# Output projection of a decoder layer: one float32 product, or three float32r products on weights and activations split into two parts

## The chip, the cores and the metric

One core of a Trainium2 chip. The metric is the device time of one execution in microseconds. Everything below is about five engines of that core and their queues: TensorE (PE, with PEld for its weight loads), VectorE (DVE), ScalarE (ACT), GpSimd (POOL) and SyncE (SP). Each engine works through its own instructions in order and waits at semaphores; SyncE, ScalarE and GpSimd also issue DMAs from their in-order queues.

## The reference

A decoder layer over x of 4 x 512 x 512 (four batch rows of 512 tokens), float32. Its first part is the one that matters here:

```
xn = layernorm(layernorm(x), g_norm)
q = xn @ Wq            # 512 -> 16 heads x 128
k, v = split(xn @ Wkv) # one key and one value head
attn = softmax(16-scaled l2norm(q) . l2norm(k))
out = attn @ v         # 16 heads x 128 = 2048 columns
out = out @ Wout       # 2048 -> 512: the output projection
x = x + layernorm(out, g_out)
```

After it come a state-space scan over ctx (16 states, 512 channels, gated by the norm of x) and a mixture of 32 experts of which each token takes up to 8.

## The kernel before, in words

The four batch rows (b or r in the code) run one after another, and the expert part follows them. For each batch row TensorE makes the queries of four groups of four heads, and for every head the scores, the weighted values and the transposed output, which ScalarE evacuates as `o_t[:, h, :]` (`transposed`, line 1075). Meanwhile VectorE runs the scan: per state n a `state_input` (line 1491), a `state_scan` (1497), a `state_product` (1504) and a `state_sum` (1509), each over 128x2048, with ScalarE making the decays. States 0 to 4 run in `start_heads`, 5 to 11 in the head groups 2 and 3 (`later_heads`, 1521), and 12 to 15 in `last_states` (1538), which runs beside the output projection.

The output projection (`out_proj`, line 750) is one function per head: four tiles of 128 tokens, each one float32 product of `o_t` with `wout`, added up over 16 heads in the four banks bank_o and bank_s. The trace has two records for a float32 product. In the batch rows 0 to 2 the next row's first stages are woven between the heads, in an order written out by hand: transposes of the norm after the heads 2 and 3, keys and values after 5, the first queries after 7, the scan's input projection after 10 and 11, `scan_params` after 12, `deltas` after 13, key transposes and the other first queries after 14. The second pair of transposes waits for the first `norm_lo` (xn_lo) of VectorE. In the last batch row the 16 heads run on end, and the layer's tail (`out_copied`, norm, gates, routing) waits for them.

The weights of the projection are kept in four places of [128, 512]. SyncE loads them (`load_wout`, line 358): four heads ahead of the projection, and the others as `wout_used` says that a place is free. SyncE also loads `b_bc` and `c_bc`, the rows B and C of the states; those of states 14 and 15 stand among the weight loads (before heads 8 and 11).

GpSimd's queue holds `load_wq` (line 1909; 1 MB a group of heads, issued when the queries before it are made, since there is one place for them) and, after the fourth group of a batch row, the 32 indirect DMAs (`send`, 1916) that write the routing of the batch row before into `lists`. The first weights of the next row's queries are loaded after those sends. At the start ScalarE splits Wq into two parts (`split_wq`, 1035) and VectorE makes the rest (1443); they are stored to DRAM and loaded back by group.

Such a split is used in the kernel in many places: ScalarE rounds a value to float32r by a copy (hi), VectorE subtracts it from the value (lo), and TensorE adds up hi x hi, hi x lo and lo x hi.

## Time and profile before

| | us |
|---|---|
| median of 3 runs | 1762.98 |
| lowest, highest | 1757.42, 1764.99 |
| span of the profiled execution | 1759.8 |
| output projection stage of batch row 0 | 277.6 to 384.0 |
| the same in batch row 1, 2 | from 600.2, from 921.3 |
| output projection of the last batch row | 1242.2 to 1298 |

The profile is of one execution. A row of the timeline names the start and the length in us, the engine, the line of the kernel, the operation, what it writes and reads with its shape, how many instructions were merged, and in brackets how long the engine was idle before it and who released it. "Busy" of TensorE is modelled at its ends, and its records overlap, so a pace is read from start to start.

### The profile page before, as it was taken

The numbers are of one execution on the slowest core, as the hardware profiler recorded it, in microseconds if no ns is written. First come the engines' busy times: TensorE is split into PE (matmuls) and PEld (weight loads), VectorE is DVE, ScalarE is ACT, GpSimd is POOL, SyncE is SP. The second block draws the span as 40 slices with busy tenths as digits, with TensorE's granted clock in tenths as the row PEclk, the third lists the DMA queues.
The fourth block names the chain that finished last, engine by engine and source line by source line (L and its number), as shares of the span: only waits on it lengthen the run. The fifth ranks groups of instructions, "written<-read, shape, count | busy, mean of one in ns | idle before, by whom it ended". The sixth has DMA issues, their size and how long they took to land. (4 is left out here: it accounts for less than half of the span.)

```text
span 1759.8 us, 25049 instructions
## 1 busy us (share of the span) xinstructions
PE 1436.2 (82%) x6762; PEld 1018.9 (58%) x6763; DVE 1245.9 (71%) x1543; ACT 941.3 (53%) x2428; POOL 499.0 (28%) x307
## 2 busy tenths in 40 slices
PE   4899888988988798898869879977863746899996
PEld 1577665446766453676755357765422535677774
DVE  5465898756699975767998468699885424667663
ACT  4666662457567335675743447766320424566662
POOL 0000000000028600000880000068301545666664
PEclk9799999989999998899989989999985878999998
DMA  6692132132332422142133124212601446999985
GB/s 236 254 262 85 40 116 85 48 97 61 97 85 65 125 73 70 45 144 72 40 98 120 50 72 124 93 38 51 206 22 52 113 110 146 224 234 241 236 204 69
DMA packets 128788, 202.45 MB, mean 115 GB/s; under 512 B 44984, under 2 KB 46473, under 8 KB 127552
## 3 DMA queue, kind: packets, MB, share of 16 engines
q1 hardware_dynamic: 75120, 86.70, 17.5%
q0 software_dynamic: 27840, 63.83, 14.9%
q10 hardware_dynamic: 25744, 50.87, 9.6%
q8 instruction: 44, 0.72, 0.2%
q14 instruction: 40, 0.33, 0.1%
HBM read 170.57 MB, written 46.21 MB: 123 GB/s over the span
## 5 line engine op out<-in xcount | busy, mean ns | idle before, releaser
L1918 POOL DMA_INDIRECT lists<-entry,slot x128 | 267.8, 2092 | 227.9 <-DVE slot L1686 190.2
L1501 DVE TENSOR_TENSOR_SCAN state<-decay,dbu 128x2048 f32<-128x2048 f32 x64 | 283.1, 4423 | 24.2 <-ACT decay L1051 22.9
L1914 POOL DMA_DIRECT2D wq<-wq_dram x30 | 21.5, 720 | 869.9 <-PE pair L581 744.2
L645 PE MATMUL bank<-v_aug,probs 128*128 128x129 f32 x2048 | 253.1, 283 | 8.1 <-ACT probs L1045 8.1
L645 PEld LDWEIGHTS bank<-v_aug,probs 128*128 128x128 f32 x2048 | 244.5, 198 | 17.2 <-ACT probs L1045 16.2
L755 PE MATMUL bank<-wout,o_t 128*128 128x512 f32 x512 | 236.1, 616 | 0.0
L1045 ACT ACTIVATE probs<-bank 128x512 f32<-128x512 f32 x256 | 145.8, 605 | 106.3 <-PE bank L627 93.3
L1051 ACT ACTIVATE decay<-delta,neg_a 128x511 f32<-128x511 f32 x256 | 164.8, 736 | 65.4 <-DVE state L1501 59.4
L755 PEld LDWEIGHTS bank<-wout,o_t 128*128 128x128 f32 x512 | 100.0, 199 | 122.5 <-issue 122.1
L1953 POOL DMA_INDIRECT out<-y_ring,add_ids x68 | 125.2, 1842 | 94.8 <-DMA out<-y_ring,add_ids 66.7
L1495 DVE TENSOR_TENSOR dbu<-du,b_bc 128x2048 f32<-128x2048 f32 x64 | 146.5, 2289 | 7.0 <-DMA c_bc<-bc_dram 5.2
L1507 DVE TENSOR_TENSOR dbu<-state,c_bc 128x2048 f32<-128x2048 f32 x64 | 146.6, 2290 | 1.9
L627 PE MATMUL bank<-q_t,k_t 128*128 128x512 f32 x256 | 128.6, 640 | 13.6 <-ACT q_t L1033 9.3
L1512 DVE TENSOR_TENSOR y<-y,dbu 128x2048 f32<-128x2048 f32 x60 | 137.4, 2290 | 1.8
L579 PE MATMUL pair<-wq,xn_hi 128*128 128x512 f32 x256 | 113.6, 444 | 20.7 <-DVE q_lo L1461 16.9
L1072 ACT ACTIVATE o_s<-bank,den 128x128 f32<-128x128 f32 x256 | 73.1, 374 | 74.1 <-DVE den L1519 74.1
L1005 ACT ACTIVATE junk<-pair 128x128 bf16<-128x128 f32 x256 | 68.1, 293 | 78.9 <-PE pair L581 78.8
L580 PE MATMUL pair<-wq,xn_hi 128*128 128x512 f32 x256 | 107.4, 420 | 0.0
L581 PE MATMUL pair<-wq,xn_lo 128*128 128x512 f32 x256 | 107.2, 419 | 0.0
L503 PE MATMUL bank<-const,o_s 128*128 128x128 f32 x272 | 47.7, 303 | 72.1 <-ACT o_s L1072 72.1
L1858 DVE TENSOR_TENSOR xt_lo<-pair,xt_hi (+1 forms) x70 | 48.1, 689 | 80.7 <-ACT xt_hi L1317 79.8
L875 PE MATMUL bank<-w_hi,xt_hi 128*128 x272 | 99.0, 364 | 6.8 <-DVE xt_lo L1858 6.6
(227 smaller groups left out, 2731.8 us busy)
## 6 DMA issues: line engine op xcount, KB each, us to landing
wq<-wq_dram POOLq DMA_DIRECT2D x30, 1024.0 KB, 8.6
w_raw<-in_w_exp ACTq DMA_DIRECT2D x32, 768.0 KB
wout<-in_wout SPq DMA_DIRECT2D x64, 256.0 KB, 2.8
b_bc<-bc_dram SPq DMA_DIRECT2D x64, 256.0 KB, 3.7
c_bc<-bc_dram SPq DMA_DIRECT2D x64, 256.0 KB, 4.6
w_raw<-in_w_exp ACTq DMA_DIRECT2D x32, 512.0 KB
lists<-in_const ACTq DMA_DIRECT2D x1, 8712.0 KB, 48.4
q_s<-in_x SPq DMA_DIRECT2D x4, 1024.0 KB, 8.1
```

What stands on the lines that cost most here:

```text
L579: pe.matmul(bank_q[t % 2][:], xn_hi[:, k, tile], wq[:, 0, k, :], start=(k == 0), stop=False)
L627: mm = pe.matmul(bank_s[k % 2][:], k_t[:, tile], q_t[:, j, :], start=True, stop=True)
L645: mm = pe.matmul(bank_o[half][:, (t % 2) * (DH + 1):(t % 2 + 1) * (DH + 1)], probs[:, k, t * P:(t + 1) * P], v_aug[:, k, :], start=(k == 0 ...
L755: mm = pe.matmul((bank_o + bank_s)[t][:], o_t[:, h, t * P:(t + 1) * P], wout[:, h % 4, :], start=(h == 0), stop=(h == H - 1))
L1045: act.activation(probs[:, k, :], bank_s[k % 2][:], ACT.Exp).then_inc(S["exp_ok"], 1)
L1051: act.activation(dA3[:, e, 1:], delta[:, e, 1:], ACT.Exp, scale=neg_a[:, bass.ds(n, 1), e:e + 1].rearrange("p a c -> p (a c)")).then_inc(S ...
L1495: dve.tensor_tensor(dbu[:], du[:], b_bc[:, i:i + 1, :].to_broadcast([P, ET, T]), ALU.mult).then_inc(S["dbu_ok"], 1)
L1501: dve.tensor_tensor_scan(state[:].rearrange("p e t -> p (e t)"), dA, dbu[:].rearrange("p e t -> p (e t)"), 0.0, ALU.mult, ALU.add).then_in ...
L1507: dve.tensor_tensor(dbu[:], state[:], c_bc[:, i:i + 1, :].to_broadcast([P, ET, T]), ALU.mult).then_inc(S["bc_free"], 1)
L1512: dve.tensor_tensor(dst[:], y[:], dbu[:], ALU.add).then_inc(S["y_ok"], 1)
L1918: pool.indirect_dma_start(out=lists, out_offset=bass.IndirectOffsetOnAxis(ap=slot[:, t, k:k + 1].bitcast(U32), axis=0), in_=entry[:, t, :] ...
L1953: pool.indirect_dma_start(out=out, out_offset=bass.IndirectOffsetOnAxis(ap=add_ids[:, r:r + 1].bitcast(U32), axis=0), in_=y_ring[:, r, :], ...
```

## The change

- The output projection takes three float32r products for each float32 product: o_hi x w_hi, o_hi x w_lo, o_lo x w_hi.
- The hi part of a head's output is a copy by ScalarE (`head_hi`) into one of five places: two new ones, and k_t, k_hi and k_lo, which are free once the scores of the batch row are made. HI_PLACE names the place, HI_BEFORE the head whose projection must be done before the place is written again. VectorE then subtracts (`head_lo`) and writes the lo part over `o_t`.
- Both stand in the order of their engines by hand. ScalarE: heads 0 and 1 after the heads 13 and 14 of the last group, 2 to 4 at its end, and the others between the steps of the stage. VectorE: heads 0 and 1 ahead of `first_norms`, 2 to 4 ahead of state 12, 5 to 11 after the scans and products of the states 12 to 15, 12 ahead of the convolution and 13 to 15 behind it.
- The weights are split once, in batch row 0. GpSimd loads them raw, ScalarE and VectorE split two heads at a time at eight places of `start_heads` (`weights_out`), GpSimd stores both parts to `wout_dram`. On GpSimd's queue `load_wq(0, 2)` stands after the store of head 6 and `load_wq(0, 3)` after that of head 13.
- The weights of a head (now 512 KB) are loaded by GpSimd, in each batch row behind the sends of the batch row before. The places are two halves of wout, and q_hi and q_lo.
- SyncE loses `load_wout`; its loads of B and C for states 14 and 15 follow at once. `load_x(0)` moves to batch row 0.
- In the last batch row two of the three expert splits move behind the projection, on ScalarE and VectorE.

```diff
@@ SyncE
-            for h in range(4):
-                load_wout(h)
...
-            load_x(0)
...
+                if b == 0:
+                    wout_stored(sp)
+                    load_x(0)
...
-                for h in range(4, H):
-                    if h in (8, 11):
-                        load_bc(b, 14 if h == 8 else 15)
-                    sp.wait_ge(S["wout_used"], b * (H - 1) + (h - 3))
-                    load_wout(h)
+                for n in range(14, DS):
+                    load_bc(b, n)
@@ TensorE, out_proj
-                pe.wait_ge(S["oT_ok"], b * H + h + 1)
+                pe.wait_ge(S["ohi_ok"], b * H + h + 1)
+                pe.wait_ge(S["olo_ok"], b * H + h + 1)
...
-                    mm = pe.matmul((bank_o + bank_s)[t][:], o_t[:, h, t * P:(t + 1) * P], wout[:, h % 4, :], start=(h == 0), stop=(h == H - 1))
+                    pe.matmul(dst, o_hi_of(h)[:, tile], w[:, 0, :], start=(h == 0), stop=False)
+                    pe.matmul(dst, o_hi_of(h)[:, tile], w[:, 1, :], start=False, stop=False)
+                    mm = pe.matmul(dst, o_lo(h)[:, tile], w[:, 0, :], start=False, stop=(h == H - 1))
@@ ScalarE
+            def head_hi(b, h):
+
+                act.wait_ge(S["oT_ok"], b * H + h + 1)
+                if HI_BEFORE[h] is not None:
+                    act.wait_ge(S["wout_used"], b * (H - 1) + HI_BEFORE[h] + 1)
+                elif HI_PLACE[h] >= 2:
+                    act.wait_ge(S["s_ps"], b * H * KT + H * KT)
+                act.activation(o_hi_of(h), o_t[:, h, :], ACT.Copy).then_inc(S["ohi_ok"], 1)
...
+            def split_wout(h):
+
+                act.wait_ge(S[f"wo_raw{h % 8}"], h // 8 * 16 + 16)
+                if h >= 4:
+                    act.wait_ge(S[f"wo_out{h % 4}"], h // 4 * 32)
+                act.activation(wout_hi(h), wout_raw(h), ACT.Copy).then_inc(S["wohi_ok"], 1)
@@ VectorE
+            def head_lo(b, h):
+
+                dve.wait_ge(S["ohi_ok"], b * H + h + 1)
+                dve.tensor_tensor(o_lo(h), o_t[:, h, :], o_hi_of(h).bitcast(F32), ALU.subtract).then_inc(S["olo_ok"], 1)
...
             def last_states(b, between):
+                for h in range(2, 5):
+                    head_lo(b, h)
                 for n in range(12, DS):
                     state_scan(b, n)
+                    head_lo(b, 2 * n - 19)
                     state_product(b, n)
+                    if n < DS - 1:
+                        head_lo(b, 2 * n - 18)
@@ GpSimd
+            load_wq(0, 1)
+            for h in range(8):
+                load_raw(h)
+            for h in range(H):
+                store_wout(h)
+                if 3 <= h < 11:
+                    load_raw(h + 5)
+                if h == 6:
+                    load_wq(0, 2)
+                elif h == 13:
+                    load_wq(0, 3)
...
+            for b in range(NB):
+                for h in range(2):
+                    load_wout(b, h)
+                if b < NB - 1:
+                    load_wq(b + 1, 0)
+                for h in range(2, H):
+                    load_wout(b, h)
+                if b == NB - 1:
+                    break
+                for group in range(1, G):
                     load_wq(b + 1, group)
```

## Rows read from the trace of the kernel before

**Rows 1.** The page's part 1: busy us (share of the span) xinstructions, by engine.
```profile
PE 1436.2 (82%) x6762; PEld 1018.9 (58%) x6763; DVE 1245.9 (71%) x1543; ACT 941.3 (53%) x2428; POOL 499.0 (28%) x307
```
**Rows 2.** Busy time by stretch: the output projection stage of batch row 0.
```profile
core 0: us, PE busy (x) PEld busy (x) DVE busy (x) ACT busy (x) POOL busy (x), PEclk, DMA share, GB/s
277.60:384.00 106.40, 97.39 (x287) 49.50 (x285) 74.39 (x70) 44.26 (x120) 1.43 (x2) 0.92 0.27 76
```
**Rows 3.** Groups of instructions, shapes apart: the projection on TensorE (busy us, mean ns).
```profile
L755 PE MATMUL bank<-wout,o_t 128*128 128x512 f32 x512 | 236.1, 616 | 0.0
```
**Rows 4.** Timeline of TensorE (start us, us): one projection head; float32r products of the queries.
```profile
290.94 3.60 PE L755 MATMUL bank<-wout,o_t 128*128 128x512 f32 x8
294.37 1.04 PE L503 MATMUL pair<-const,probs 128*128 128x128 f32 x8
...
451.84 0.40 PE L580 MATMUL pair<-wq,xn_hi 128*128 128x512 f32 x1
452.07 0.39 PE L581 MATMUL pair<-wq,xn_lo 128*128 128x512 f32 x1
```
**Rows 5.** Timeline of VectorE, projection stage of batch row 0: its pauses.
```profile
279.16 0.16 DVE L1381 SCALAR_TENSOR_TENSOR rs_t<-rs_x,rs_yy 128x4 f32<-128x4 f32 x1 [0.99 <-ACT rs_yy L943]
...
295.73 1.41 DVE L1451 SCALAR_TENSOR_TENSOR xn_lo<-pair,g_norm,xn_hi 128x512 fp32r<-128x512 f32 x2 [1.64 <-ACT xn_hi L954]
298.75 4.42 DVE L1501 TENSOR_TENSOR_SCAN state<-decay,dbu 128x2048 f32<-128x2048 f32 x1 [1.60 <-ACT decay L1051]
...
312.41 4.42 DVE L1501 TENSOR_TENSOR_SCAN state<-decay,dbu 128x2048 f32<-128x2048 f32 x1 [1.20 <-ACT decay L1051]
...
328.82 4.42 DVE L1501 TENSOR_TENSOR_SCAN state<-decay,dbu 128x2048 f32<-128x2048 f32 x1 [4.73 <-ACT decay L1051]
...
368.16 1.23 DVE L1476 TENSOR_SCALAR dbu<-decay 128x2048 f32<-128x2048 f32 x1 [20.40 <-ACT du L998]
```
**Rows 6.** Timeline of ScalarE, the same stage: four copies of 128x512.
```profile
381.14 2.11 ACT L1092 ACTIVATE o_t<-bank 128x512 f32<-128x512 f32 x4
```
**Rows 7.** Timelines of GpSimd, VectorE and TensorE, first head groups of batch row 0.
```profile
119.07 1.43 POOL L1914 DMA_DIRECT2D wq<-wq_dram  x2 [42.78 <-PE pair L581]
...
134.66 1.29 DVE L1461 TENSOR_TENSOR q_lo<-pair,q_hi 128x512 fp32r<-128x512 f32 x2 [7.06 <-ACT q_hi L1033]
...
137.59 0.47 PE L579 MATMUL pair<-wq,xn_hi 128*128 128x512 f32 x1
```
**Rows 8.** DMA: lists' filling (KB, us to landing); landing of the wq loads at 119.07.
```profile
lists<-in_const ACTq DMA_DIRECT2D x1, 8712.0 KB, 48.4
...
DMA to landing us min/median/max: 14.7/15.7/16.6
```
**Rows 9.** Timelines of TensorE and GpSimd where batch row 1's projection starts.
```profile
600.27 11.70 PE L755 MATMUL bank<-wout,o_t 128*128 128x512 f32 x24
...
602.67 1.57 POOL L1914 DMA_DIRECT2D wq<-wq_dram  x2
```
**Rows 10.** Landing of the two wq loads at 602.67, from the tile's view.
```profile
DMA to landing us min/median/max: 6.7/8.0/9.3
```
**Rows 11.** Timelines of the five engines, projection stage of the last batch row.
```profile
1241.06 4.16 POOL L1918 DMA_INDIRECT lists<-entry,slot  x1 [0.30 <-issue]
1245.53 2.09 POOL L1918 DMA_INDIRECT lists<-entry,slot  x1 [0.30 <-issue]
...
1242.19 56.23 PE L755 MATMUL bank<-wout,o_t 128*128 128x512 f32 x128
...
1242.44 6.26 ACTq L1227 DMA_DIRECT2D w_raw<-in_w_exp  x4
...
1295.88 0.60 ACT L1092 ACTIVATE o_t<-bank 128x512 f32<-128x512 f32 x1 [18.31 <-PE bank L755]
...
1240.01 4.42 DVE L1501 TENSOR_TENSOR_SCAN state<-decay,dbu 128x2048 f32<-128x2048 f32 x1
...
1265.84 2.29 DVE L1495 TENSOR_TENSOR dbu<-du,b_bc 128x2048 f32<-128x2048 f32 x1 [5.25 <-DMA c_bc<-bc_dram]
...
1279.74 4.42 DVE L1501 TENSOR_TENSOR_SCAN state<-decay,dbu 128x2048 f32<-128x2048 f32 x1
```

More of the change, by code:

```diff
@@ L164, in sb, with both @@
             return stage_a.enter_context(nc.sbuf_tensor(name, shape, dt))
+        def both(name, shape):
+            with ExitStack() as place:
+                plain = place.enter_context(nc.sbuf_tensor(name, shape, F32))
+            return plain, sb(name + "_r", shape, F32R)
         wq = sb("wq", [P, 2, KT, GROUP], F32R)
@@ L307, in wq_stored, with wout_stored @@
                 eng.wait_ge(S[f"wq_out{g}"], 2 * 16)
+        def wout_stored(eng):
+            for i in range(4):
+                eng.wait_ge(S[f"wo_out{i}"], 4 * 2 * 16)
         def more_blocks(eng, e):
@@ L438, in row @@
                 first_bc(b + 1)
-                sp.wait_ge(S["op_ps"], b * TT + TT)
-                for h in range(4):
-                    load_wout(h)
                 start_heads(b + 1, b)
@@ L1116, in start_heads, with weights_out @@
                                   a["const"][:, C_ALL:].unsqueeze(1).to_broadcast([P, NE + 1, PADS * LIST_COLS])).then_inc(S["lists_in"], 16)
+                def weights_out(h):
+                    if not tail:
+                        split_wout(2 * h)
+                        split_wout(2 * h + 1)
                 exps_divide(row, 0)
@@ L1187, in third_group @@
                 next_squares(row, 2, 0, at)
+                if row == 0:
+                    wout_stored(act)
                 act.wait_ge(S["carry_ok"], row)
@@ L1223, in last_group @@
                         decays(row, h - 2)
+                    if h in (13, 14):
+                        head_hi(row, h - 13)
+                for h in range(2, 5):
+                    head_hi(row, h)
             def load_part(e, part):
@@ L1693, in start_heads, with weights_out @@
                 tail = b is not None
+                def weights_out(h):
+                    if not tail:
+                        split_wout(2 * h)
+                        split_wout(2 * h + 1)
                 if tail:
@@ L1767, in row @@
                     last_states(b, lambda n: None)
+                    for h in range(12, H):
+                        head_lo(b, h)
                     dve.wait_ge(S["oT_ok"], NB * H)
-                    for e in range(2):
-                        for part in range(2):
-                            split(e, part)
+                    for part in range(2):
+                        split(0, part)
                     out_stats(b, at)
@@ L1776, in row @@
                     gate_norm(b, at)
+                    for part in range(2):
+                        split(1, part)
                     gated(b)
@@ L1798, in row @@
                 last_states(b, between)
+                head_lo(b, 12)
                 convolution(b + 1, link)
+                for h in range(13, H):
+                    head_lo(b, h)
                 deltas(b + 1, link)
@@ L1925, in _, with load_raw, store_wout, load_wout @@
                     pool.dma_start(out[NTOK + row:NTOK + row + rows, :], a["x"][row:row + rows, :]).then_inc(S[f"added{parity}"], 16)
-            wq_stored(pool)
-            for group in range(1, G):
-                load_wq(0, group)
-            for b in range(NB - 1):
-                for group in range(G):
+            def load_raw(h):
+                if h >= 8:
+                    pool.wait_ge(S[f"wo_out{h % 4}"], (h - 8) // 4 * 32 + 32)
+                pool.dma_start(wout_raw(h), a["wout"][h * DH:(h + 1) * DH, :]).then_inc(S[f"wo_raw{h % 8}"], 16)
+            def store_wout(h):
+                pool.wait_ge(S["wohi_ok"], h + 1)
+                pool.wait_ge(S["wolo_ok"], h + 1)
+                for part, src in ((0, wout_hi(h).bitcast(F32)), (1, wout_raw(h))):
+                    pool.dma_start(wout_dram[h][:, part], src).then_inc(S[f"wo_out{h % 4}"], 16)
+            wq_stored(pool)
+            load_wq(0, 1)
[9 more added lines that the diff above has]
+                    load_wq(0, 3)
+            wout_stored(pool)
+            def load_wout(b, h):
+                if h == 2:
+                    pool.wait_ge(S["s_ps"], b * H * KT + H * KT)
+                if h >= 4:
+                    pool.wait_ge(S["wout_used"], b * (H - 1) + (h - 3))
+                elif b > 0:
+                    pool.wait_ge(S["op_ps"], b * TT)
+                pool.dma_start(wout_of(h)[:], wout_dram[h]).then_inc(S[f"wout_in{h % 4}"], 16)
+            for b in range(NB):
+                for h in range(2):
+                    load_wout(b, h)
[6 more added lines that the diff above has]
+                for group in range(1, G):
                     load_wq(b + 1, group)
```

66 lines of the change are left out of this document (58 added, 8 removed).

## The prediction

> **What bounds the kernel now.** I read the page's engine totals first: TensorE is busy for 82% of the span, VectorE for 71%, ScalarE for 53% [rows 1]. Such shares say little about one stage, so the next view is the one by stretches. In the output projection of batch row 0 (277.6 to 384.0 us) TensorE is busy for 97.4 of 106.4 us at a granted clock of 0.92, and VectorE for 74.4 [rows 2]. That looks bound by TensorE. The waits of VectorE say otherwise [rows 5]. From the first norm to the end of the scan's last state it has five pauses: 0.99, 1.64, 1.60, 1.20 and 4.73 us. Only two of them lead back to TensorE. The 1.64 before the third xn_lo is in part the fourth projection head ahead of the transposes, and the 1.20 before the scan at 312.41 is keys and values, queued behind projection heads. The 4.73 at 328.82 is VectorE's own doing: ScalarE scales the queries and makes the decays only after a Newton step that stands behind VectorE's state work. Then come 20.40 us in which VectorE waits for the delta chain (silu, w_x, deltas, Exp, Ln), and one projection head lies inside that chain. So VectorE and the chains that it starts set this stage's length, and TensorE runs beside them with little slack. In the last batch row the reverse holds: 128 records of the projection run from 1242.19 for 56.23 us, VectorE's last scan starts at 1279.74, and ScalarE waits 18.31 us for the projection's result [rows 11].
>
> **What the change gives.** One head of the projection (4 tiles, 8 records in float32) takes 294.37 - 290.94 = 3.43 us; a float32r product of the same 128x128 by 128x512 starts 0.23 us after the one before it, so 12 of them take 2.76 [rows 4]. That is 0.67 us a head and 43 us of 236.1 busy us [rows 3] over 64 heads, of which row by row only what TensorE holds up can be seen in the time.
>
> **What it costs on the engines.** Per head ScalarE makes a copy of 128x512 (four take 2.11 us, so 0.5 each) [rows 6], and VectorE a subtraction (two take 1.29 us, 0.65 each and about 0.6 where they follow one another) [rows 7]. VectorE's place in the order decides. Heads 0 to 4 stand ahead of the scan of state 12, heads 5 to 10 between the steps of states 12 to 14, 11 and 12 in state 15 and ahead of the convolution: 13 subtractions of 0.6 on its path, +7.8. Heads 13 to 15 fall into the 20.40 us pause: nothing, and +0.6 each if that cover were gone. TensorE's gain takes back about 1.0 of the 1.64 and 1.60, and the 1.20, say -2.0. Inside the delta chain head 13 is 0.7 shorter, and ScalarE's copy of head 15 stands between Exp and Ln, +0.5. Out-projection of batch row 0: 7.8 - 2.0 - 0.7 + 0.5 = 5.6, **+6** (3 to 9: all waits recovered, or none and 0.65 each). TensorE would now wait for VectorE's first xn_lo before its second pair of transposes, by about 7 us: that xn_lo comes some 4.2 us later (seven subtractions) and TensorE is 4 x 0.67 = 2.7 earlier.
>
> **What moves to GpSimd's queue.** The weights (now 512 KB a head, two parts) no longer go by SyncE, where four heads lie ready before the stage begins. They stand behind load_wq and the 32 sends of the batch row before, on an in-order queue. In batch row 1 the sends are done and the queue is free at 602.67, while the projection starts at 600.27 [rows 9]. Two 512 KB transfers issued there land 6.7 and 9.3 us after their issue [rows 10]. So head 0's weights land at 609.4, 9 us after TensorE could begin. Head 2's stand behind head 1's and the 1 MB of wq, near 617. Queued behind this: ScalarE's copy of head 5 waits for wout_used 1, and VectorE's subtraction for that copy, within state 12; the first transposes of the next row stand behind head 2 and VectorE's xn_lo behind them. The 7 us of slack found above hide most of it. I find +1.4 at the subtraction of head 5, +2.3 at the first xn_lo, +3.9 at the third: **+10** for each of the rows 1 and 2 (6 to 15; the low end is the sum of row 0, the high end has every transfer land 3.3 us after the one before it, 9.3 - 6.7 and 0.7 between the two issues).
>
> By the Trainium skill, DMA: Bandwidth & Descriptors, section "Anatomy of one DMA — SWDGE (gpsimd) path", a transfer from GpSimd's queue takes about 2.0 us and its bytes at 436 GB/s, 3.2 us for 512 KB as an estimate; the first one here took 6.7 [rows 10], so the row disagrees. By the page batch rows 1 to 3 would each be some 3 us shorter than I say, 1817 in all.
>
> **The last row** [rows 11]. The last send starts at 1245.53 and takes 2.09, so head 0's weights land near 1254.3 and its projection ends near 1258.5 (2.76, and 1.4 more for a part at the lower of the two clock levels after a pause; the mean of 0.92 in rows 2 leaves room for that). Only then come the copies of heads 5 and 6, ahead of the decays of state 13. The copy also stands behind four expert loads that take 6.26 us to issue. VectorE's scan of state 12 starts at 1240.01 and would start at 1245.2 (five subtractions, waiting for the copies); its product now waits for head 5 until about 1259.6, and was due at 1244.5: +15. The 5.25 us wait for c_bc at 1265.84 goes, since the SyncE queue no longer holds that load behind the weights; five more subtractions add 2.8. So the scan of state 15 moves from 1279.74 to about 1292. It ends at 1296.4; head 11, product, sum and head 12 end at 1302; TensorE then has the heads 12 to 14 (8.3 us) and a tile of head 15 (0.7) to do before ScalarE can copy, at 1311 and not at 1295.88: +15. The 11 us by which the products of this row are shorter (16 x 0.67) are lost behind VectorE. Expert splits, which lay in TensorE's shadow, now stand in the tail: ScalarE's ahead of the norm seed (+0.8) and VectorE's ahead of the gating (+1.3). **+17** (9 to 20; 9 with weights there in time).
>
> **The split of the weights in row 0.** 16 raw loads, 16 copies, 16 subtractions, 32 stores. Most of the copies and subtractions fall into pauses of the first head groups, where VectorE waits for TensorE, as 7.06 us at 134.66 [rows 7]. Two pairs of copies stand directly ahead of what TensorE waits for (+1.0 each) and one pair of subtractions ahead of the stretch that VectorE bounds (+1.2). The queue is worse. load_wq of group 2 is issued at 119.07 today; now it stands behind the store of head 6, whose parts are split only after the q_lo at 134.66. TensorE wants these queries at 137.59 [rows 7]. So it is issued near 139, with stores and raw loads ahead of it on its own queue. And the DMA is full at that time: the 8.7 MB filling of lists takes 48.4 us from 87.9, and the wq load beside it took 14.7 and 16.6 us to land [rows 8]. With 5 MB more to move by then, I take 154 for the landing, 16 us after TensorE wants it; load_wq of group 3 is some 1 us late. TensorE is the engine that the others wait for there, so all counts: 16 + 2.0 + 1.2 + 1 = **+20** (12 to 28: an unhindered landing in 9 us, or a queue backlog of another 8).
>
> **Sum.** 20 + 6 + 10 + 10 + 17 = 63 us. The profiled execution's span is 1759.8 us, and its row would become 1823; the median of the three runs is 1762.98, 3.2 above that span, and what lies around it is left as it is. Predicted: 1763 + 63 = 1826 us. All low ends give +36 and all high ends +87.
>
> **Rivals.** (a) The weight loads of rows 1 to 3 are in time or nearly: the sends end only 2.4 us after the stage begins, and TensorE has slack. Then 4 + 4 + 7 us less: 1811. Against it stand the landing times. 10%. (b) The wq load of row 0 isn't waited for: 1810. For it: the DMA could drain sooner. Against: the order of the queue is fixed by the stores. 14%. (c) GpSimd's transfers are held up by VectorE. Sends take 4.16 us at 1241.06, beside a scan, and 2.09 elsewhere [rows 11]. If each weight load were held so, a head's weights would come every 4.2 us, more than 2.76, and the three rows would gain 16 x 1.4 less their slack, some 8 each: 1850. Against it: the wq loads issue at 0.7 us each, beside VectorE's work too [rows 7]. [...] 8%. (d) The other side: TensorE bounds all four stages, the subtractions and copies fall into VectorE's 10 us of pauses, and loads and stores are hidden. It decides if fewer than 3 of the 13 subtractions lengthen VectorE's path and wq comes by 138. Then rows 0 to 2 gain 2 each and the last 9: 1748. For it only TensorE's 97.4 of 106.4 us. 4%. (e) The new products don't run at 0.23 us but at the 0.39 to 0.40 of one record's length [rows 4]: 4.7 us a head, TensorE leads again and rows grow by 15 more: 1870. Products back to back show 0.23. 2%. My forecast: 62%.
>
> **Chances and range.** 0.5% (8.8 us) is about what this measurement can tell from no change. Faster by more: (d), 4%, and 1% for what I don't see. Within: 5%, if (a) and (b) hold together and the order costs less than I think. Slower: 90%. The range 1795 to 1850 takes in (a), (b) and (c) and the low ends almost together.
>
> **What would show it.** In the changed profile: TensorE pauses before the first queries of group 2 (near 138) for a wq load; a pause at the start of the projection in rows 1 to 3 for weights loaded by GpSimd; the projection's records at 0.23 us; a scan of state 15 that starts some 6 to 12 us later after the stage's start than now; no wait for c_bc in the last row; out_copied some 15 us later in it. I am wrong if wq lands by 140, if VectorE's path doesn't grow by the subtractions, or if the weights are there at the stage's start.

## The result and the profile after

The changed kernel takes 1830.36 us, median of 4 runs (1825.54 to 1835.66), against 1762.85 us for the kernel before: ratio 1.038, 95% interval 1.034 to 1.042. The profiled execution has a span of 1830.9 us, 71.1 more than 1759.8. The forecast was 1826 us and a range of 1795 to 1850. The sum was nearly right; two of its terms were not, with opposite signs.

The page's part 1 of the changed kernel answers to [rows 1]; below it stand two of the groups with shapes apart, VectorE's subtraction and the first product where its left part comes from `o_hi` (busy us, mean ns | idle before and what ended it):

```profile
PE 1427.8 (78%) x7018; PEld 1089.2 (59%) x7019; DVE 1291.9 (71%) x1623; ACT 982.8 (54%) x2508; POOL 558.3 (30%) x419
...
L770 PE MATMUL bank<-wout,o_hi 128*128 128x512 f32 x48 | 22.6, 470 | 19.0 <-DMA wout<-wout_dram 19.0
...
L1596 DVE TENSOR_TENSOR o_t_r<-o_t,o_hi 128x512 fp32r<-128x512 f32 x32 | 21.4, 681 | 78.5 <-ACT o_hi L1103 78.5
```

TensorE is busy for 8.4 us less, not for 43 less; behind the new pauses part of its products run at the slower of two paces, as shown below. VectorE has 46 us more, ScalarE 41.5, GpSimd 59. The row at L770 shows the first pauses that were not there before: the projection waits 19.0 us for weights.

To see where the 71.1 us came from I cut both spans at the same events: `skip` of a row done, the last `den` of the row's heads, the next `skip`, ScalarE's first copy of the last projection (`out_copied`), and the last `carry`. All times below come from the timelines of VectorE and ScalarE at these events; "stage" is the stretch of the projection, from the last `den` to the `skip` of the next row, in the last row to `out_copied`. In us:

| kernel | heads row 0 | stage row 0 | stage row 1 | stage row 2 | stage, last row | tail to carry | span |
|---|---|---|---|---|---|---|---|
| before | 187.65 | 106.06 | 105.12 | 104.73 | 56.06 | 52.05 | 1759.8 |
| changed | 202.80 | 112.97 | 123.96 | 122.02 | 69.02 | 54.10 | 1830.9 |
| difference | +15.15 | +6.91 | +18.84 | +17.29 | +12.96 | +2.05 | +71.1 |

What the table leaves out (the start, the heads of rows 1 to 3, the experts) comes to -2.1: the start is 1.14 shorter and the rest is -1.0. SyncE no longer loads four heads' weights in the start; no run tests whether that is why, and among the kernels with this same start the end of the first `skip` varies by 1.5 us.

**Heads of row 0.** GpSimd issues the queries' weights of group 2 behind the store of head 6. From the timelines of GpSimd, TensorE and VectorE (start us, duration), the lines that answer to [rows 7], and the landing of that load from the tile's view, which answers to [rows 8]:

```profile
138.62 1.42 POOL L2023 DMA_DIRECT2D wq<-wq_dram  x2
...
DMA to landing us min/median/max: 7.9/9.0/10.0
...
146.69 0.77 PE L591 MATMUL pair<-wq,xn_hi 128*128 128x512 f32 x1 [8.92 <-DMA wq<-wq_dram]
147.26 0.63 PE L592 MATMUL pair<-wq,xn_hi 128*128 128x512 f32 x1
147.68 0.63 PE L593 MATMUL pair<-wq,xn_lo 128*128 128x512 f32 x1
...
151.19 0.39 PE L592 MATMUL pair<-wq,xn_hi 128*128 128x512 f32 x1
151.42 0.40 PE L593 MATMUL pair<-wq,xn_lo 128*128 128x512 f32 x1
...
160.51 0.17 DVE L1591 RECIPROCAL den<-bank 128x2 f32<-128x2 f32 x1 [15.86 <-PE bank L657]
```

TensorE starts these products at 146.69, 9.1 later than in [rows 7], and then starts ten of the twelve 0.43 us apart, until about 151 (granted clock 0.50, 1.2 GHz); from there on it has its other pace, 0.23 (granted clock 1.00, 2.4 GHz). VectorE is behind both: 15.86 us with nothing to do.

**Stage of row 1.** The timelines of GpSimd, TensorE, ScalarE and VectorE, the lines that answer to [rows 9] and [rows 5]; the third line is the landing of the first two weight loads:

```profile
623.08 0.98 POOL L2027 DMA_INDIRECT lists<-entry,slot  x1 [0.30 <-issue]
624.04 1.19 POOL L2067 DMA_DIRECT2D wout<-wout_dram  x2
DMA to landing us min/median/max: 3.9/4.3/4.7
...
628.04 0.77 PE L770 MATMUL bank<-wout,o_hi 128*128 128x512 f32 x1 [6.26 <-DMA wout<-wout_dram]
...
639.25 0.76 PE L770 MATMUL bank<-q_hi,k_t_r 128*128 128x512 f32 x1 [3.49 <-DMA q_hi<-wout_dram]
...
643.65 1.04 PE L515 MATMUL pair<-const,probs 128*128 128x128 f32 x8
...
644.29 1.27 ACT L971 ACTIVATE xn_hi<-pair,g_norm 128x512 fp32r<-128x512 f32 x2 [10.52 <-PE pair L515]
645.44 0.63 ACT L1103 ACTIVATE o_hi<-o_t 128x512 fp32r<-128x512 f32 x1
...
633.80 0.69 DVE L1596 TENSOR_TENSOR o_t_r<-o_t,o_hi 128x512 fp32r<-128x512 f32 x1 [0.31 <-ACT o_hi L1103]
634.41 2.28 DVE L1579 TENSOR_TENSOR dbu<-state,c_bc 128x2048 f32<-128x2048 f32 x1
646.11 0.69 DVE L1596 TENSOR_TENSOR o_t_r<-o_t,o_hi 128x512 fp32r<-128x512 f32 x1 [9.41 <-ACT o_hi L1103]
```

The last send ends at 624.04 and only then are head 0's weights issued. The cost is taken twice: TensorE waits for heads 0 and 2, and VectorE stands 9.41 us between two operations of state 12, for the copy of head 6. The chain can be followed in the lines: head 2 starts at 639.25, when its weights are there; the first transposes of the next row's norm stand behind it on TensorE (643.65); ScalarE scales these (644.29) and only then copies head 6 (645.44), and VectorE's subtraction follows at 646.11. Row 2 shows the same (TensorE 5.11 and 3.41, VectorE 8.39), the last row 7.62 and 6.25.

### The profile page after: what moved, and what is told of

It reads as the page before. It is cut to its first block and busy times, and to the rows that moved or that the text cites. A ratio compares the mean times of both kernels' runs of the same rounds, so it can differ in the third digit from the quotient of the medians.

```text
span 1830.9 us, 25871 instructions
## 1 busy us (share of the span) xinstructions
PE 1427.8 (78%) x7018; PEld 1089.2 (59%) x7019; DVE 1291.9 (71%) x1623; ACT 982.8 (54%) x2508; POOL 558.3 (30%) x419
## 5 line engine op out<-in xcount | busy, mean ns | idle before, releaser
L639 PE MATMUL bank<-q_t,k_t 128*128 128x512 f32 x256 | 132.7, 658 | 16.4 <-ACT q_t L1050 11.3
L2094 POOL DMA_INDIRECT x_blk<-xf_dram,get_ids x70 | 83.6, 1194 | 61.1 <-issue 28.3
L1642 DVE TENSOR_TENSOR w_lo<-w_raw,w_hi (+1 forms) x64 | 95.4, 1492 | 7.2 <-ACT w_hi L1284 5.3
```

Source lines behind the costliest of these rows:

```text
L639: mm = pe.matmul(bank_s[k % 2][:], k_t[:, tile], q_t[:, j, :], start=True, stop=True)
```

## The experiments

Each kernel is compared with the kernel before, run beside it on the same chip (medians of 1765.5 to 1766.8 us there). The first three mend GpSimd's queue; the others leave out or move the splits, or change the number of products.

**1. The queries' weights earlier.**

```diff
-                if h == 6:
+                if h == 3:
                     load_wq(0, 2)
```

> Changed kernel with one edit: on GpSimd's queue the load of the queries' weights of group 2 stands behind the store of head 3 of the output weights, not of head 6, so it is issued near 120 us and not at 138.6. Theory (the queue's order delays it, and TensorE is what the others wait for there): TensorE's wait of 8.92 us before the first product of group 2 goes, and some of the 1.4 us that these products lost at the lower clock; 9 to 11 us less, 1830.4 - 10 = 1820 us (ratio 1.033 to the kernel before). Rival (the DMA queues are full with the filling of lists, so an early issue lands no earlier than 146): 0 to 3 us less, 1828 to 1830. Second rival (the copies and subtractions of the weight split set that stretch): also 0 to 3 us, but with no wait of TensorE for wq in the trace.

Measured: 1820.04 us (1816.03 to 1824.98), ratio 1.029 (1.022 to 1.035). The load is issued at 118.33 and lands 17.6 and 20.9 us later. The heads of row 0 take 192.31 us, 10.5 less than in the changed kernel. From TensorE's timeline:

```profile
129.32 3.86 PE L639 MATMUL bank<-q_t,k_t 128*128 128x512 f32 x8 [1.79 <-ACT q_t L1050]
...
140.01 0.50 PE L591 MATMUL pair<-wq,xn_hi 128*128 128x512 f32 x1 [0.51 <-DMA wq<-wq_dram]
```

So the order of the queue was the cause, and the whole wait had counted. It is a close thing: issued 20.3 us sooner, the two halves land only 10.6 and 9.4 us sooner, just in time. The second rival falls with it; the split's copies are still there (the 1.79 us before the products with `q_t`), and worth far less.

**2. The output weights earlier.**

```diff
-                for h in range(2):
-                    load_wout(b, h)
+                if b == 0:
+                    for h in range(2):
+                        load_wout(b, h)
...
-                for h in range(2, H):
+                for h in range(2 if b == 0 else 4, H):
                     load_wout(b, h)
...
+                for h in range(2):
+                    load_wout(b + 1, h)
                 for group in range(1, G):
                     load_wq(b + 1, group)
...
                     for k in range(TOPK):
+                        if t * TOPK + k == TT * TOPK - 3:
+                            for h in range(2, 4):
+                                load_wout(b + 1, h)
                         send(t, k, S["sent"])
```

> Changed kernel with one edit: in batch rows 1 to 3 GpSimd issues the output weights of heads 0 and 1 a whole row ahead (right behind head 15 of the row before), and those of heads 2 and 3 ahead of the last three sends. Theory (late weights plus VectorE's own subtractions make the stage longer): TensorE's waits of 6.26 and 3.49 us (row 1), 5.11 and 3.41 (row 2), 7.62 (row 3) go, ScalarE's copies come sooner, and VectorE's waits of 9.41, 8.39 and 6.25 us before the subtraction of head 6 fall to 2 or less. The stages of rows 1 and 2 then grow by about 8 us over the kernel before, as row 0's did (6.9), and not by 18.8 and 17.3; the last by about 8 and not 15. 10 + 10 + 7 = 27 us less: 1803 us (ratio 1.023). Rival (the waits only cover VectorE's own order, which comes out the same): 2 to 3 us a row, 1822 us (1.034).

Measured: 1811.95 us (1806.19 to 1818.03), ratio 1.023 (1.016 to 1.029), where the rival had 1.034. The median fell by 18 us; I had expected 27, the rival 8. The stages of rows 1 and 2 take 114.48 and 114.38, that is 9.4 and 9.7 over the kernel before, and the last 63.13 (+7.1). In row 1 TensorE no longer waits for weights, and VectorE's two subtractions beside state 12 follow without a pause (VectorE's timeline):

```profile
634.25 0.66 DVE L1596 TENSOR_TENSOR o_t_r<-o_t,o_hi 128x512 fp32r<-128x512 f32 x1
...
637.04 0.68 DVE L1596 TENSOR_TENSOR o_t_r<-o_t,o_hi 128x512 fp32r<-128x512 f32 x1
```

The three stages lose 9.5, 7.6 and 5.9 us against the changed kernel. That is how much the late weights had cost. The 18 us of the median are less than these 23; in the profiled execution 2.3 us of the difference are a longer tail (last section), and the expert part behind it, whose code is the same, took 3.2 us longer.

**3. Both.**

> The edits of the two kernels before it together. Theory: the two gains lie in different stretches and add up, 1830.4 - 10 - 27 = 1793 us (ratio 1.017): still slower than the kernel before, since the subtractions on VectorE's path stay. Rival (with the order of GpSimd's queue mended, TensorE's 43 us of shorter products come through): at or below the kernel before, 1763 or less.

Measured: 1801.65 us (1795.19 to 1802.62), ratio 1.017 (1.010 to 1.023). Heads of row 0 192.96, stages 113.50, 113.85, 114.33 and 62.87. The gains lie in different stretches and add up (10 and 18 us of the medians alone, 29 together), though the sum stays 9 us short of what I expected, as experiment 2 did. 7 to 10 us a stage remain that no queue explains. The kernels that follow are all built on this one.

**4. No subtraction.**

```diff
-                pe.wait_ge(S["olo_ok"], b * H + h + 1)
...
-                    mm = pe.matmul(dst, o_lo(h)[:, tile], w[:, 0, :], start=False, stop=(h == H - 1))
+                    mm = pe.matmul(dst, o_hi_of(h)[:, tile], w[:, 0, :], start=False, stop=(h == H - 1))
...
             def head_lo(b, h):
+                return
```

> The kernel with both early loads, and VectorE's 64 subtractions are left out (the third product reads the high part of the head's output again, so the low part is missing in the result). ScalarE's 64 copies and TensorE's 12 products a head stay. Theory (the price is the subtractions in VectorE's order): 13 x 0.6 = 7.8 us less in each of the first three rows and about 6 in the last, 1801.7 - 29 = 1773 us (ratio 1.001), and the other 8 us to the kernel without copies belong to ScalarE's copies and their waits. Rival (the copies, and the waits for the places they are written to, are the price; VectorE merely waits for them): 1795 us or more (1.013).

Measured: 1768.21 us (1765.63 to 1797.89), ratio 0.999 (0.995 to 1.004). The total is as expected, its shares are not: the stages are 3.7, 6.4, 5.0 and, in the last row, 16.0 us shorter than with the subtractions, where 7.8, 7.8, 7.8 and 6 were expected. In the first three rows a part of the 7.8 falls into waits that VectorE had anyway. These are its pauses before the scans in row 0, with and without the subtractions (VectorE's timeline, the lines that answer to [rows 5]); first the kernel with both early loads:

```profile
308.72 4.42 DVE L1573 TENSOR_TENSOR_SCAN state<-decay,dbu 128x2048 f32<-128x2048 f32 x1 [2.21 <-ACT decay L1068]
...
339.37 4.42 DVE L1573 TENSOR_TENSOR_SCAN state<-decay,dbu 128x2048 f32<-128x2048 f32 x1 [4.72 <-ACT decay L1068]
```

and then this one:

```profile
305.00 4.42 DVE L1572 TENSOR_TENSOR_SCAN state<-decay,dbu 128x2048 f32<-128x2048 f32 x1 [2.21 <-ACT decay L1067]
...
319.16 4.42 DVE L1572 TENSOR_TENSOR_SCAN state<-decay,dbu 128x2048 f32<-128x2048 f32 x1 [1.71 <-ACT decay L1067]
...
335.57 4.42 DVE L1572 TENSOR_TENSOR_SCAN state<-decay,dbu 128x2048 f32<-128x2048 f32 x1 [4.73 <-ACT decay L1067]
```

The scan of state 14 waits 1.71 us here and not at all with the subtractions, and the first norm of the stage waits 2.55 us here and 1.34 with them. In the last row it is the other way: the subtractions cost more than their own time, since TensorE waits for them. TensorE's timeline in the kernel with both early loads:

```profile
1306.85 0.77 PE L770 MATMUL bank<-wout,k_lo 128*128 128x512 f32 x1 [6.62 <-issue]
...
1319.30 0.77 PE L770 MATMUL bank<-q_lo,o_hi 128*128 128x512 f32 x1 [5.24 <-issue]
```

Heads 9 and 11 start there within 0.8 us of VectorE's subtraction for them (1306.08 and 1318.53), each behind a scan of 4.42 us. Five heads are then still to do at the end of the last scan. Without the subtractions TensorE has no such pause.

**5. The last row's subtractions closer together.**

```diff
                 for n in range(12, DS):
                     state_scan(b, n)
-                    head_lo(b, 2 * n - 19)
+                    head_lo(b, 3 * n - 31 if last else 2 * n - 19)
                     state_product(b, n)
-                    if n < DS - 1:
-                        head_lo(b, 2 * n - 18)
+                    if last or n < DS - 1:
+                        head_lo(b, 3 * n - 30 if last else 2 * n - 18)
...
+                        if last:
+                            head_lo(b, 3 * n - 29)
```

ScalarE's copies of heads 5 to 8 stand ahead of the decays of state 13 here, those of 9 to 11, 12 and 13, and 14 and 15 behind the decays of 13, 14 and 15.

> The kernel with both early loads, and in the last batch row the 11 subtractions of heads 5 to 15 stand closer together: three behind each of the scans 12, 13 and 14 and two behind scan 15 (before: two a state and four behind the last sum), ScalarE's copies ahead of them to match. Nothing is left out. Theory (in the last row the price is that TensorE waits 6.62 and 5.24 us for the subtractions of heads 9 and 11 behind scans, and has five heads to do after the last scan; the subtractions' own time is the smaller part): about 8 us less, 1801.7 - 8 = 1794 us (ratio 1.012), still slower than the kernel before. Rival (the 13 subtractions' time itself is the price): no change, 1802 us.

Measured: the last stage takes 56.30 us against 62.87, so 6.6 of the 16 were the place of the subtractions, or of ScalarE's copies, which this edit moves with them. The other 9.4 stay unseparated. TensorE's two pauses are 2.45 and 4.29 now. The whole time, 1798.03 us (1795.52 to 1803.29), ratio 1.018 (1.011 to 1.025), cannot tell this from no change: the expert part of its profiled execution took 417.4 us, where that of the kernel with both early loads took 410.0 with the same code. The stage's length is the evidence, not the total.

**6. No copies either.**

```diff
-                pe.wait_ge(S["ohi_ok"], b * H + h + 1)
+                pe.wait_ge(S["oT_ok"], b * H + h + 1)
...
-                act.activation(o_t[:, h, :], bank_t[1][:], ACT.Copy).then_inc(S["oT_ok"], 1)
+                act.activation(o_lo(h), bank_t[1][:], ACT.Copy).then_inc(S["oT_ok"], 1)
...
             def head_hi(b, h):
+                return
```

> The kernel with both early loads, and the heads' outputs are not split: ScalarE's copy out of PSUM writes o_t rounded to float32r and all three products read it, so the 64 copies and 64 subtractions of 128x512 are left out (and with them the low part of the heads' outputs in the result). TensorE does the same 12 products a head. Theory (VectorE's order bounds the stages, TensorE's gain lies beside it): the 13 subtractions of 0.6 us go from each row's path and the last row's copies and waits with them, 33 to 38 us less than the kernel with both early loads: about 1757 us (ratio 0.997; 0.993 to 1.000), of TensorE's 43 us only some 6 net of the 5 that row 0's split of the weights costs. Rival (TensorE bounds the stages once the splits are gone): 1763 + 5 - 43 = 1725 us (0.978). Second rival (the copies and subtractions cost little, the rest is elsewhere): 1785 or more.

Measured: 1759.20 us (1756.93 to 1777.01), ratio 0.996 (0.992 to 1.000). Stages 106.26, 104.14, 104.31: those of the kernel before within 1 us, though TensorE's projection is 16 x 0.67 = 10.7 us shorter in each. The last is 46.80, 9.3 shorter than before. Against the kernel without subtractions alone, the copies cost 3.5, 3.4, 5.1 and 0.1. So the copies with what waits for them, for which I had counted next to nothing in row 0, are almost as dear there as the subtractions.

**7 and 8. More and less work for TensorE.** With 16 products a head, and with 8, each against the kernel of experiment 6:

```diff
                     pe.matmul(dst, o_lo(h)[:, tile], w[:, 1, :], start=False, stop=False)
+                    pe.matmul(dst, o_lo(h)[:, tile], w[:, 1, :], start=False, stop=False)
```

> The kernel without splits of the heads' outputs, with 16 products a head in place of 12 (the low part of the weights is added twice): the projection then takes TensorE 16 x 0.23 = 3.68 us a head, 0.25 more than the float32 products of the kernel before and 59 us more in all than with 12. Theory (what TensorE gained or loses in batch rows 0 to 2 lies beside VectorE's work, and counts in the last row alone): 1 to 2 us in each of the rows 0 to 2, 10 in the last, 1759 + 14 = 1773 us (ratio 1.004). Rival (TensorE bounds all stages): 1759 + 59 = 1818 us (1.030).

```diff
-                    pe.matmul(dst, o_lo(h)[:, tile], w[:, 1, :], start=False, stop=False)
-                    mm = pe.matmul(dst, o_lo(h)[:, tile], w[:, 0, :], start=False, stop=(h == H - 1))
+                    mm = pe.matmul(dst, o_lo(h)[:, tile], w[:, 1, :], start=False, stop=(h == H - 1))
```

> The kernel without splits of the heads' outputs, with 8 products a head in place of 12: the rounded head by the high and by the low part of the weights (what is left out is the low part of the heads' outputs). TensorE has 64 x 4 x 0.23 = 59 us less to do. Theory (VectorE and its chains bound batch rows 0 to 2; in the last row VectorE is done 3 us before TensorE): 0 in rows 0 to 2, 3 us in the last, 1756 us (ratio 0.994). Rival (TensorE bounds the stages): up to 14 us a row, 1715 us (0.971).

Measured: 1771.92 us (1768.90 to 1797.39), ratio 1.004 (1.001 to 1.008), and 1753.58 us (1746.39 to 1763.13), ratio 0.992 (0.988 to 0.996). In us:

| products a head | stage row 0 | stage row 1 | stage row 2 | stage, last row |
|---|---|---|---|---|
| 16 | 106.86 | 104.59 | 104.60 | 59.99 |
| 12 | 106.26 | 104.14 | 104.31 | 46.80 |
| 8 | 103.53 | 103.91 | 104.09 | 42.20 |

A step of 4 products is 16 x 0.92 = 14.7 us of TensorE's time a row. In rows 1 and 2 it moves the stage by 0.2 to 0.5, in row 0 by 0.6 up and 2.7 down. In the last row the step up costs 13.2 of 14.7 and the step down gives 4.6. I had put the end of that gain down to VectorE's last scan; TensorE's timeline with 8 products says otherwise:

```profile
1256.78 0.74 PE L769 MATMUL bank<-wout,o_t_r 128*128 128x512 f32 x1 [4.04 <-DMA wout<-wout_dram]
...
1267.98 0.47 PE L769 MATMUL bank<-wout,o_t_r 128*128 128x512 f32 x1 [1.96 <-DMA wout<-wout_dram]
```

With 0.40 and 0.78 at two more heads it waits 7.2 us for weights, whose four places it now empties faster than they are filled. These two kernels are the plainest evidence of the study: TensorE bounds the last stage, and none of the other three by more than a small part.

**9. The weights not split.** On the kernel of experiment 6; stores and loads stay, the 16 copies and 16 subtractions of row 0 go.

```diff
             def split_wout(h):
+                return
...
-                pool.wait_ge(S["wohi_ok"], h + 1)
-                pool.wait_ge(S["wolo_ok"], h + 1)
-                for part, src in ((0, wout_hi(h).bitcast(F32)), (1, wout_raw(h))):
+                pool.wait_ge(S[f"wo_raw{h % 8}"], h // 8 * 16 + 16)
+                for part, src in ((0, wout_raw(h)), (1, wout_raw(h))):
```

> The kernel without splits of the heads' outputs, and the weights' 16 copies on ScalarE and 16 subtractions on VectorE in batch row 0 are left out as well: GpSimd stores the raw weights twice (so the low part of the weights is wrong in the result), the transfers stay as they are. Theory (row 0's remaining 7 us over the kernel before are those copies and subtractions standing ahead of others' work): 4 to 6 us less, 1759 - 5 = 1754 us (ratio 0.993). Rival (they are the 16 loads and 32 stores, which slow other transfers): no change, 1759 us (0.996).

Measured: 1754.50 us (1749.19 to 1765.56), ratio 0.993 (0.989 to 0.996); the heads of row 0 take 189.13 us against 194.53, 5.4 less. TensorE's waits of 1.80 us for `q_t` at two places have fallen below 0.8. The theory holds, but the 5.4 is a rough size: TensorE's waits for wq are 1.3 us shorter here (1.16 against 0.58 and 1.85), and seven kernels that split the weights and have the wq load at this place (that of experiment 10 left aside) took 191.9 to 194.5 us for these heads, their mean 4.1 above 189.13. What is left over the kernel before is 189.13 - 187.65 = 1.5 us, and TensorE's remaining wait for wq is 1.16 of it.

**10. The subtractions on GpSimd.**

```diff
+            def pool_lo(b, h):
+                pool.wait_ge(S["ohi_ok"], b * H + h + 1)
+                pool.tensor_tensor(o_lo(h), o_t[:, h, :], o_hi_of(h).bitcast(F32), ALU.subtract).then_inc(S["olo_ok"], 1)
...
+                for h in range(0 if b == 0 else 2, 4):
+                    pool_lo(b, h)
+                for h in range(4, H):
+                    load_wout(b, h)
+                    pool_lo(b, h)
```

> The kernel with both early loads, with the 64 subtractions of heads moved from VectorE to GpSimd, each just behind the load of the weights of that head or of one some places on. Nothing is left out of the result. Theory (VectorE's order is the price, and GpSimd is idle there but for sends and loads): VectorE's order is that of the kernel without subtractions; TensorE waits for a subtraction here and there. 1773 us and 0 to 15 more: 1780 (ratio 1.004). Rival (work on GpSimd and VectorE holds each other up, as the sends at 4.16 us beside a scan and 2.09 elsewhere suggest): VectorE's operations, or GpSimd's, grow by as much as was moved, 1800 us or more (1.016).

Measured: 1808.83 us (1805.51 to 1811.44), ratio 1.023 (1.016 to 1.030), 7 us more than with the subtractions on VectorE. The rival is right. GpSimd's and VectorE's timelines in row 1, the same stretch:

```profile
627.99 3.32 POOL L2072 TENSOR_TENSOR o_t_r<-o_t,k_hi 128x512 fp32r<-128x512 f32 x1
...
638.42 1.30 POOL L2072 TENSOR_TENSOR o_t_r<-o_t,o_hi 128x512 fp32r<-128x512 f32 x1
...
627.00 3.17 DVE L1579 TENSOR_TENSOR dbu<-state,c_bc 128x2048 f32<-128x2048 f32 x1
630.20 3.25 DVE L1584 TENSOR_TENSOR y<-y,dbu 128x2048 f32<-128x2048 f32 x1
```

A subtraction takes GpSimd 1.30 us where VectorE is idle or works on PSUM and 2.7 to 3.4 beside VectorE's products, which go from 2.29 to 3.2 us. Beside a scan that ends at 680.11 one takes 4.98, from 676.21 to 681.19. By the page's part 1, VectorE is busy for 1296.7 us, 41 more than without subtractions (1255.3), though it does none; with them it was 1291.9. The 37 us that VectorE lost in subtractions came back as longer operations, and TensorE waits for the slower results besides (2.18 us at 628.12, for head 2). The Trainium skill, SBUF — State Buffer, section "SBUF: two separate sides", describes a port pair that the two engines share under a lock, which an operation of VectorE with two inputs in SBUF and one of GpSimd that reads SBUF take in turn. The rows agree with that: the subtraction beside the scan ends 1.08 us after it.

**11. Two products, and the splits moved.** Of kernels that leave out only the low part of the heads' outputs, the best I found: as with 8 products, ScalarE's copies of the weights of heads 4, 5, 12 and 13 behind the scaled queries, and the wq load behind the store of head 1, where it stood behind that of head 3.

```diff
-                weights_out(2)
                 decays(row, 2)

                 q_transposed(row, 1, 0)
+                weights_out(2)
```

> The kernel with two products a head (low part of the heads' outputs left out), with two moves in batch row 0: ScalarE's copies of the weights of heads 4, 5 and 12, 13 stand behind the first scaled queries of the next group and not ahead of them, and the load of the queries' weights of group 2 ahead of the stores of heads 2 and 3. Theory (these are what TensorE waits for there, 1.80 us twice and 1.85 once, against 0.8 and 0 without them): 2 to 3 us less, 1751 us (ratio 0.990). Rival (TensorE then waits for the exponentials behind the moved copies): no change, 1753.6 us (0.992).

Measured: 1748.21 us (1741.88 to 1759.06), ratio 0.990 (0.987 to 0.994); heads of row 0 190.50 against 194.05, the waits for `q_t` 0.76. TensorE's wait of 1.92 us for wq of group 2 is gone; one of 3.10 for that of group 3, at 187.64, is new. The whole time can't tell this kernel from that of experiment 8 (the intervals overlap); the heads of row 0 can, being 1.3 us below the lowest of the seven kernels named in experiment 9. It is faster than both the kernel before and the changed one, but it is no answer to the change: its result carries the heads' outputs rounded to float32r. With all three terms no kernel here was faster than the one before; the best ratio is 1.017.

## Why the prediction was right, and where it was not

**TensorE is not what the stages wait for: right.** The 43 us of shorter products were to show in part in the last row only. The kernels with 16, 12 and 8 products confirm it. Rival (d), that TensorE bounds all four stages, is out: with 8 products the first three become 0.2 to 2.7 us shorter and not 14.7.

**Row 0's stage, +6: measured 6.9, by another working.** I had 7.8 for 13 subtractions less 2.0 and 0.7 of waits recovered and 0.5 for a copy. Subtractions net of the waits they fall into are 3.7, the copies 3.5, and the shorter products give back about nothing (106.26 against 106.06). The forecast held since the term for the copies was too small and the one for the subtractions too large. The first xn_lo: TensorE was to wait about 7 us for it, and waited 6.74 at 311.68.

**Rows 1 and 2, +10 each: measured 18.8 and 17.3.** This is the step that failed. The place was right, the size not. The sends ended where I had them, 2.3 us after TensorE's wait began. The landing was shorter than I took it, 4.0 us from issue to the first product and not 6.7, for a reason that stood in the page: I read the transfers of [rows 10] as 512 KB each, and they are 1024. The page's part 6 of the changed kernel has both sizes (KB each, us to landing):

```profile
wq<-wq_dram POOLq DMA_DIRECT2D x30, 1024.0 KB, 8.5
...
wout<-wout_dram POOLq DMA_DIRECT2D x32, 512.0 KB, 4.1
```

So a `load_wq` brings 2 MB a group of heads, and not the 1 MB of the description of the kernel. That error alone would have made my term too large. It came out too small since I had priced only the copy of head 5 (+1.4) and the xn_lo (+2.3, +3.9). The +10 does not follow from these either: they come to 7.6, and with row 0's 5.6 to 13.2. I missed that the copy of head 6 stands behind the first pair of scaled transposes, these behind head 2, and this behind its weights: 9.41 us inside state 12. Experiment 2 puts the late weights at 9.5 and 7.6 us, and what remains, 9.4 and 9.7, is splits: 7 to 8 that row 0's stage has too (6.9 in the changed kernel, 8.2 in that of experiment 2), and 1 to 3 more of which I know only that they go with the splits (104.14 and 104.31 without them).

**Rival (c), and the landing of a transfer.** GpSimd's weight loads issue in 0.53 us each and none of the 64 takes over 0.64, though 14 of them are issued wholly inside a scan of VectorE. All 22 sends of 3.9 us or more in the kernel before lie beside a scan. So plain loads were not held up as the sends are; (c) is out for them. For arithmetic on GpSimd it is real (experiment 10). The estimate of 3.2 us by the Trainium skill, DMA: Bandwidth & Descriptors, section "Anatomy of one DMA — SWDGE (gpsimd) path", is nearer to the 4.0 measured for 512 KB than my 6.7 was. I had held it against the row of a transfer twice as large. For that size the same rule gives an estimate of 4.4 us, and the row still has 6.7. It changed little, since the delay came from the queue and the chain, not from the transfer.

**The last row, +17: measured 13.0 in the stage and 2.1 in the tail, 15.0.** Weights late (7.62), copies of heads 5 and 6 late (6.25 at VectorE), no wait for c_bc, expert splits in the tail: all are in the trace as described. I had `out_copied` at 1311 against 1295.88, so +15; it is 69.6 later, of which 56.7 came from ahead, so +13.0. The weights were there 4 us sooner than forecast after the stage's start (1306.67, where 1254.3 and the 56.7 make 1311.0), for the most part by the same error of size; and the first head's products took 5.12 us, where I had 2.76 and 1.4 for the lower clock, a term that no row had shown. What I saw only for head 11 is that the subtractions behind scans feed TensorE too slowly. Experiments 4 and 5 size it: 16.0 us for the subtractions, 6.6 of them by their place and that of the copies.

**The weight split in row 0, +20: measured 14.0** (15.15 less the 1.14 of the earlier start). The queue's order was right to the place: issue at 138.62 forecast as "near 139", a wait of TensorE for wq. The term that was mis-sized is the landing: 154 forecast, 146.7 measured. I had carried over the 14.7 to 16.6 us of [rows 8] to a load issued 20 us later; it took 7.9 to 10.0. The filling of the lists was over at 139.8, 1.2 us after the issue, which fits the shorter landing and the 17.6 to 20.9 us of the load issued at 118.33 beside it; no run separates it from the other transfers. Two things were added that I did not have: ten products at the slower pace behind the pause (0.2 us each, 2 in all), and the splits' own cost came out at 4 to 5 (experiment 9) where I had 3.2 with two places out of three named rightly.

**The sum.** Over by 6 in the heads of row 0, under by 1 in its stage and by 16 in rows 1 and 2, over by 2 in the last, and 1 us of small gains not forecast: 63 + 8 = 71. The right total rests in part on errors that cancelled, and only experiments 1 and 2 tell which terms were earned.

## What to carry to other kernels

Before a cheaper form of an operation is priced, find the stages in which its engine ends the wait; here that was one of four stages, and 43 us of TensorE's time bought some 9. What the new form needs from other engines is paid at their place in the order: 13 subtractions of 0.6 us cost 4 to 6 us in three stages and 16 in the fourth, where TensorE waited for them, and a load moved behind an in-order queue of sends cost 6 to 10 us a row until it was issued a row ahead. When a wait is added, follow it through every queue to the last engine that stands behind it, since the largest term that I missed was a copy three queues away from the late transfer.

## What the runs showed that I had not expected

**The 32 products of the gate ran in 4.31 or in 7.04 us**, with the same instructions. In the kernels before and changed they start at the lower clock and go over to the higher; in the kernel without splits of heads, with both early loads and others they stay at the lower (granted clock 0.50, 1.2 GHz) to their end. The timeline of TensorE and the busy time by stretch, first before:

```profile
1330.18 4.31 PE L787 MATMUL bank<-w_gate,o_t 128*128 128x32 f32 x32 [0.75 <-ACT o_t L1087]
1322.00:1335.00 13.00, 8.21 (x48) 7.18 (x48) 3.05 (x14) 3.04 (x8) 0.00 (x0) 0.63 0.33 123
```

and without splits of heads:

```profile
1327.31 7.04 PE L803 MATMUL bank<-w_gate,o_t 128*128 128x32 f32 x32 [0.75 <-ACT o_t L1120]
1319.00:1335.00 16.00, 10.93 (x48) 9.91 (x48) 3.32 (x14) 3.04 (x8) 0.00 (x0) 0.50 0.28 103
```

(the last numbers of a row by stretch are the granted clock, the DMA share and GB/s). In both TensorE had done two groups of 16 transposes, 3.9 us long each, in the 16 us before (granted clock 0.50 from 1310 to 1322 in the kernel before). What decides which way it goes I can't say, and each kernel has one profiled execution. The tail is 2.3 us longer in the kernels of experiments 2, 3 and 6 than in the changed one (56.4 against 54.1), against their gains. It works the other way for 8 products a head: there the gate's products took 4.35 us, so 2.7 of the 4.9 us that this kernel gains from the last `den` to the last `carry` are the clock's and not the step's.

**A load's landing time follows what else is under way.** The same two transfers of wq landed in 14.7 to 16.6 us, 7.9 to 10.0 and 17.6 to 20.9, as issued at 119.07, 138.62 and 118.33 in three kernels.

**GpSimd and VectorE pay for each other's arithmetic**: 37 us of subtractions moved off VectorE lengthened its other operations by 41 (busy 1291.9, 1255.3 and 1296.7 us with them, without them and with them on GpSimd).
